# A convolution by pairs of images: the last pair computed with row products too, and work dealt out anew among VectorE, ScalarE and GpSimd

## The chip, the cores and the metric

One core of one Trainium2 chip. The metric is device time in microseconds of one execution of the whole kernel; lower is better.

## The reference

The input `x` has 32 images of 64 channels of 56 x 56 numbers, in float32. The weights `W` are 64 x 64 x 3 x 3, and only their signs are used.

```
bw  = sign(W)
g   = x.reshape(32, 32 groups, 2 channels, 56, 56)
xn  = (g - mean(g over channels, rows, columns)) / sqrt(var(g) + 1e-5)
out = x + conv2d(xn, bw, 3x3, stride 1, padding 1)
```

So each group of two neighbouring channels of an image is normalised by itself, convolved with weights of +1 and -1, and added to the input.

## The kernel before

**Pairs.** The 32 images are 16 pairs (`k` from 0 to 15, `LAST` is 15). A pair fills the 128 partitions, 64 channels of each image. It lies in one of `XRING` = 8 slots of `xbuf`, where the result is added in place and from where it is stored.

**Normalising.** For a pair, VectorE takes `bn_stats` of seven blocks (L500), combines them (`aggregate`, L502) and makes the factor and the offset (`scale`, L513), with a square root from ScalarE (`deviation`, L411) between. ScalarE then writes the scaled pair twice, as float16 (`hi`, L421, into `halves`) and as float32 (`normalise`, L415, into `xnorm`). GpSimd subtracts the one from the other (`lo`, L326), which gives a second float16 half, so that the convolution keeps its precision with float16 matmuls. This is done by chunks of rows (`chunks`, L132): two per pair, 29 and 27 rows in an ordinary pair. `halves` has three slots, `xnorm` two.

**Convolution.** TensorE runs 64x64 weight tiles, four at a time. A block of up to 9 rows takes 9 taps for the upper half and then 9 for the lower, added up in one PSUM bank. *Home* blocks write an image's result to its own partitions, *away* blocks to the other image's: rows are shared out between the two so that all four quarters of the array work. A block starts with the nine taps of the upper half, and waits for the lower one only then (`wait_lower`, L695). Home blocks use PSUM banks 0 to 3, away blocks 4 to 7, in units of two banks; a block of unit `u` waits in `wait_bank` (L669) until the unit `u - 2` on its side has been read out.

**Products.** In the pairs of `WINOGRAD` (L30: 3, 6, 9, 12, 14) the 18 rows 25 to 42 are computed as 9 couples of rows by four row products of three taps each, in place of 18 rows by nine taps. Their inputs are the lines STEP (even row minus odd), SUM (odd plus even) and DIFF (rows two apart), made by GpSimd from the raw input (`make_lines`, L347), scaled twice by ScalarE (`line_upper`, L440, into `line_halves` and `lines_norm`) and subtracted by GpSimd (`lo_lines`, L363). The other 13 home rows are ordinary blocks, 25 rows are away. Such a pair has chunks of 26 and 14 rows, since rows between are needed only as lines. In L78 the unit of the 13 rows comes first, then products 2 and 1, then 0 and 3.

**Taking the result out.** VectorE adds home blocks from PSUM to `xbuf` (`add_home` L546; `add_inner` L589 and `add_outer` L602 for the products). An away unit goes one of two ways (`by_scalar`, L115): VectorE adds it in two operations of 64 partitions (`add_away`, L559), or ScalarE moves it across partitions to `moved` (`move_away`, L427) and GpSimd adds it (`add_away`, L333). Before the change the second unit of an ordinary pair and the first of a product pair go by ScalarE and GpSimd, the rest by VectorE.

**Order.** Each engine's program is written out by hand, pair by pair, and runs in order; engines meet at counting semaphores. VectorE works on statistics two pairs ahead. SyncE issues all loads and stores, three in flight (`load`, `paced_store`), with those of the last pair after L308. TensorE deals a pair's home and away steps alternately by columns done (L746). In the last pair the blocks get narrower towards the end (L76, L83), so that little is left to add and store after the last matmul.

## Time and profile before

| | us |
|---|---|
| median of 3 runs | 201.85 (201.57 to 202.32) |
| span of the profiled execution | 200.7 |
| PE busy | 191.2 (95%) |
| DVE busy | 165.3 (82%) |
| ACT busy | 149.7 (75%) |
| POOL busy | 166.7 (83%) |
| granted TensorE clock | 1.00 of full speed |

The span runs from the first instruction to the last of one profiled execution, and is 1.15 us shorter than the median of the runs. PE is TensorE, DVE is VectorE, ACT is ScalarE and POOL is GpSimd. PEld is TensorE's loading of weights, which runs beside its matmuls. In rows of the trace, L followed by a number is a line of the kernel, `out<-in` names the tiles, and the bracket at the end says how long the engine had stood idle before and what ended that.

### The profile page before, as it was taken

Reading aid. Unit: us, or ns where it says so; the run is one execution under the profiler, and the core shown is the slowest. Engines: PE = TensorE matmul, PEld = TensorE weight load, DVE = VectorE, ACT = ScalarE, POOL = GpSimd, SP = SyncE. Lnnn points to the kernel's source line nnn. Section 1 sums busy time; section 2 is a strip of 40 time slices with the busy share of each in tenths; the row PEclk is TensorE's granted clock in tenths of the full one; section 3 lists DMA queues with packets and bytes.
Section 4 is the critical chain, followed back from the end, with each engine's and each line's share of the span. In section 5 each row is a group of like instructions: output and inputs, shape, how many; then the busy total and the mean of one; then the engine's idle time right before and its main releaser. Section 6 shows DMA issues by size and latency. Waiting matters only on the chain.

```text
span 200.7 us, 10042 instructions
## 1 busy us (share of the span) xinstructions
PE 191.2 (95%) x4482; PEld 168.4 (84%) x4482; DVE 165.3 (82%) x363; ACT 149.7 (75%) x142; POOL 166.7 (83%) x85
## 2 busy tenths in 40 slices
PE   1999999999999999999999999999999999999990
PEld 0478888879858988988999988899998999889990
DVE  2799999996999997799988779998779999627392
ACT  3185999799989289899909989972998999595000
POOL 1029786999999999999999997999999899999500
PEclk9999999999999999999999999999999999999999
DMA  6978977871787988868697887868887883906274
GB/s 216 362 217 292 331 246 252 289 209 44 306 243 291 297 316 282 282 248 278 242 301 296 275 327 276 325 228 321 326 241 296 266 319 152 381 13 238 116 283 175
DMA packets 18698, 52.17 MB, mean 260 GB/s; under 512 B 2080, under 2 KB 5024, under 8 KB 18656
## 3 DMA queue, kind: packets, MB, share of 16 engines
q1 hardware_dynamic: 18656, 51.54, 72.9%
q8 instruction: 35, 0.57, 1.1%
q14 instruction: 7, 0.06, 0.1%
HBM read 25.84 MB, written 25.69 MB: 257 GB/s over the span
## 4 chain that ended last, share of the span: by engine, by line
PE 65%; ACT 14%; DVE 13%; DMA 3%; issue 1%; SPq 0%; DVEq 0%; ACTq 0%
PE psum L738 65%; ACT halves L424 5%; DVE stats L500 5%; ACT xnorm L418 4%; DMA xbuf<-in_x_dram 3%; ACT moved L437 3%; DVE xbuf L570 2%; DVE xbuf L556 1%; DVE xbuf L580 1%; DVE own L508 1%; ACT line_halves L447 1%; ACT std L413 1%; DVE xbuf L544 1%; ACT lines_norm L451 1%; DVE halves L538 1%
## 5 line engine op out<-in xcount | busy, mean ns | idle before, releaser
L738 PE MATMUL psum<-halves,w_taps 64*64 64x385 f16 (+8 forms) x4140 | 183.4, 325 | 0.5 <-DVE halves L532 0.4
L738 PEld LDWEIGHTS psum<-halves,w_taps 64*64 64x64 f16 x4140 | 156.7, 107 | 19.3 <-ACT moved L437 0.9
L330 POOL TENSOR_TENSOR halves<-xnorm,halves 128x784 f16<-128x784 f32 (+5 forms) x35 | 91.6, 2637 | 20.0 <-ACT xnorm L418 19.7
L500 DVE BATCH_NORM_STATS2 stats<-xbuf 128x6 f32<-128x448 f32 x112 | 60.8, 613 | 4.3 <-DMA xbuf<-in_x_dram 4.1
L424 ACT ACTIVATE halves<-xbuf,coef 128x784 f16<-128x784 f32 (+5 forms) x35 | 50.7, 1449 | 3.0 <-DVE coef L525 2.8
L418 ACT ACTIVATE xnorm<-xbuf,coef 128x784 f32<-128x784 f32 (+5 forms) x35 | 50.5, 1443 | 0.0
L437 ACT ACTIVATE moved<-psum 64x784 f32<-64x784 f32 (+1 forms) x30 | 25.5, 850 | 7.9 <-PE psum L738 7.3
L345 POOL TENSOR_TENSOR xbuf<-xbuf,moved 128x784 f32<-128x784 f32 (+1 forms) x15 | 29.3, 1956 | 0.4 <-ACT moved L437 0.4
L570 DVE SCALAR_TENSOR_TENSOR xbuf<-psum,xbuf 64x784 f32<-64x784 f32 (+1 forms) x32 | 28.2, 881 | 1.0
L556 DVE SCALAR_TENSOR_TENSOR xbuf<-psum,xbuf 128x784 f32<-128x784 f32 x21 | 20.3, 967 | 7.6 <-PE psum L738 7.4
L371 POOL TENSOR_TENSOR line_halves<-lines_norm,line_halves 128x1512 f16<-128x1512 f32 (+1 forms) x10 | 20.9, 2120 | 0.5 <-ACT lines_norm L451 0.5
L738 PE MATMUL psum<-line_halves,w_products 64*64 64x504 f16 (+1 forms) x180 | 20.8, 373 | 0.0
L587 DVE SCALAR_TENSOR_TENSOR xbuf<-psum,xbuf 128x504 f32<-128x504 f32 x30 | 18.6, 673 | 1.5 <-PE psum L738 1.5
L413 ACT ACTIVATE std<-own,eps 128x1 f32<-128x1 f32 x16 | 4.6, 287 | 14.8 <-DVE own L508 14.8
L358 POOL TENSOR_TENSOR lines<-xbuf 128x1008 f32<-128x1008 f32 x5 | 11.7, 2337 | 0.0
L651 PE MATMUL psum<-filler 64*64 64x448 f16 x84 | 7.3, 508 | 4.2 <-DMA xbuf<-in_x_dram 4.2
L544 DVE SCALAR_TENSOR_TENSOR xbuf<-psum,xbuf 128x392 f32<-128x392 f32 (+3 forms) x13 | 6.2, 508 | 5.9 <-PE psum L738 5.8
L738 PEld LDWEIGHTS psum<-line_halves,w_products 64*64 64x64 f16 x180 | 10.0, 107 | 0.7
L651 PEld LDWEIGHTS psum<-filler 64*64 64x64 f16 x84 | 3.5, 154 | 7.1 <-DMA xbuf<-in_x_dram 4.2
L508 DVE BATCH_NORM_AGGREGATE own<-stats 128x2 f32<-128x84 f32 x16 | 8.5, 534 | 0.6
L517 DVE RECIPROCAL inv<-std 128x1 f32<-128x1 f32 x16 | 2.6, 161 | 7.1 <-ACT std L413 7.1
L451 ACT ACTIVATE lines_norm<-lines,coef 128x1512 f32<-128x1512 f32 x5 | 7.7, 1542 | 0.0
(36 smaller groups left out, 72.0 us busy)
## 6 DMA issues: line engine op xcount, KB each, us to landing
xbuf<-in_x_dram SPq DMA_DIRECT2D x48, 448.0 KB, 4.6
out_dram<-xbuf SPq DMA_DIRECT2D x43, 392.0 KB, 4.0
xbuf<-in_x_dram SPq DMA_DIRECT2D x16, 224.0 KB, 4.1
out_dram<-xbuf SPq DMA_DIRECT2D x5, 504.0 KB, 3.9
out_dram<-xbuf SPq DMA_DIRECT2D x5, 448.0 KB, 3.8
out_dram<-xbuf SPq DMA_DIRECT2D x5, 364.0 KB, 4.1
out_dram<-xbuf SPq DMA_DIRECT2D x5, 252.0 KB, 4.1
out_dram<-xbuf SPq DMA_DIRECT2D x1, 224.0 KB, 3.8
```

What stands on the lines that cost most here:

```text
L330: nc.gpsimd.tensor_tensor(at(halves[:, k % HRING, 1, :], a, b), at(xnorm[:, k % NRING, :], a, b), at(halves[:, k % HRING, 0, :], a, b), AL ...
L345: nc.gpsimd.tensor_tensor(away, away, part, ALU.add).then_inc(add_done, 1)
L358: nc.gpsimd.tensor_tensor(lines[:, DIFF], at(xbuf[:, s, :], WROW - 1, WROW + WROWS - 1), at(xbuf[:, s, :], WROW + 1, WROW + WROWS + 1), AL ...
L371: nc.gpsimd.tensor_tensor(line_halves[:, 1, some], lines_norm[:, some], line_halves[:, 0, some], ALU.subtract).then_inc(line_lo_ready, 1)
L418: nc.scalar.activation(at(xnorm[:, k % NRING, :], a, b), at(xbuf[:, s, :], a, b), ACT.Identity, bias=coef[:, s, 1:2], scale=coef[:, s, 0:1 ...
L424: nc.scalar.activation(at(halves[:, k % HRING, 0, :], a, b), at(xbuf[:, s, :], a, b), ACT.Identity, bias=coef[:, s, 1:2], scale=coef[:, s, ...
L437: nc.scalar.mul(moved[here, m % 2, 0:len(unit) * size].rearrange("p (n m) -> p n m", m=size), psum[there, bank:bank + len(unit), 0:size], ...
L500: nc.vector.bn_stats(stats[:, n, :], xbuf[:, s, n * STAT:(n + 1) * STAT]).then_inc(blocks_ready, 1)
L556: nc.vector.scalar_tensor_tensor(both_rows, psum[:, bank:bank + 2, 0:BN], 1.0 / SCALE, both_rows, ALU.mult, ALU.add).then_inc(home_done, 1)
L570: nc.vector.scalar_tensor_tensor(part[here], made[there], 1.0 / SCALE, part[here], ALU.mult, ALU.add).then_inc(away_done, 1)
L587: return nc.vector.scalar_tensor_tensor(part, made, factor / SCALE, part, ALU.mult, ALU.add)
L738: mm = pe.matmul(outs[:, :, left:right], weights, ins[:, :, left + dx:right + dx], start=first_step, stop=last_step)
```

## The change

It has four parts.

1. **The last pair is a product pair** (`WINOGRAD` gets 15). Its home units are 7 rows, products 2 and 1, products 0 and 3, then 3 and 3 rows; its away units 16, 6 and 3 rows. Its stores are cut to match, and its chunks are 26 and 14 rows.
2. **Lines.** SUM is made by VectorE (`sum_line`), with twice the mean taken off in the same operation, so that all four quarter lines are scaled in one operation of 2016 elements. They are scaled in place (no `lines_norm`), and `lines` and `line_halves` are double. In pairs 14 and 15 VectorE makes the lower half of the lines itself, in one operation that also scales (`lo_lines` of VectorE); in the others GpSimd does, in one operation of 2016 elements where there were two of 1512 and 504.
3. **Away units.** All go by ScalarE and GpSimd, except those in `BY_VECTOR` and the last pair's. On both engines the add or move of a pair's first unit stands between the two chunks of the next pair (after them, if that is a product pair).
4. **VectorE's order.** The seven blocks of statistics are spread around the additions (4 and 3, or 2, 2 and 3), and `aggregate` comes after `add_inner` in a product pair.

`SCALAR_BLOCKS` is empty, so `stats_by_scalar` issues nothing and all statistics stay with VectorE.

```diff
-WINOGRAD = (3, 6, 9, 12, 14)
+WINOGRAD = (3, 6, 9, 12, 14, 15)
+LINES_BY_VECTOR = (14, 15)
+BY_VECTOR = {(0, 0), (1, 0), (13, 1), (14, 0), (14, 1)}
+SCALAR_BLOCKS = {}
...
     def home_units(k):
         if k == LAST:
-            return [[(0, 7), (14, 7)], [(28, 7), (42, 4)], [(50, 3)]]
+            return [[(WROW + WROWS, 7)], [2, 1], [0, 3], [(WROW + WROWS + 7, 3)], [(WROW + WROWS + 10, 3)]]
...
     def away_units(k):
         if k == LAST:
-            return [[(7, 7), (21, 7)], [(35, 7), (46, 4)], [(53, 3)]]
+            return [[(0, 8), (8, 8)], [(16, 6)], [(22, 3)]]
...
     def by_scalar(k, i):
-        return k != LAST and i == (0 if k in WINOGRAD else 1)
+        return k != LAST and (k, i) not in BY_VECTOR
...
 (SyncE, store_unit)
+                if k == LAST:
+                    wait_away(k, 0)
+                    store(k, 0, 0, 16)
+                    sp.wait_ge(home_done, home_before(k) + 3)
+                    store(k, 1, WROW, WROW + WROWS + 7)
+                    sp.wait_ge(home_done, home_before(k) + 4)
+                    wait_away(k, 1)
+                    store(k, 2, 16, 22)
+                    store(k, 3, WROW + WROWS + 7, WROW + WROWS + 10)
+                    sp.wait_ge(home_done, home_before(k) + 5)
+                    store(k, 4, WROW + WROWS + 10, H)
+                    wait_away(k, 2)
+                    sp.dma_start(at(both(out, k), 22, WROW),
+                                 at(xbuf[:, k % XRING, :], 22, WROW)).then_inc(last_stored, 16)
+                    return
...
 (GpSimd, make_lines)
-                nc.gpsimd.tensor_tensor(lines[:, SUM].rearrange("p (r w) -> p r w", w=W), odd, even,
-                                        ALU.add).then_inc(lines_made, 1)
...
 (GpSimd, lo_lines)
-                for i, some in enumerate((slice(0, 3 * WN), SUM)):
-                    pool.wait_ge(line_hi_ready, 2 * n + i + 1)
-                    pool.wait_ge(line_norm_ready, 2 * n + i + 1)
-                    nc.gpsimd.tensor_tensor(line_halves[:, 1, some], lines_norm[:, some], line_halves[:, 0, some],
-                                            ALU.subtract).then_inc(line_lo_ready, 1)
+                pool.wait_ge(line_norm_ready, lines_before(k + 1, False))
+                nc.gpsimd.tensor_tensor(line_halves[:, n % 2, 1, :], lines[:, n % 2, :], line_halves[:, n % 2, 0, :],
+                                        ALU.subtract).then_inc(line_lo_pool, 1)
...
 (GpSimd, the loop over pairs)
             for k in range(NP):
-                if k >= 2 and k - 2 not in WINOGRAD and k != WINOGRAD[0]:
+                if k >= 2 and by_scalar(k - 2, 1):
                     add_away(k - 2, 1)
-                for c in range(len(chunks(k))):
+                last = len(chunks(k)) - 1
+                for c in range(last):
                     if (k, c) != (0, 0):
                         lo(k, c)
+                if k in WINOGRAD:
+                    lo(k, last)
+                if k >= 1 and by_scalar(k - 1, 0):
+                    add_away(k - 1, 0)
+                if k not in WINOGRAD:
+                    lo(k, last)
+                elif k not in LINES_BY_VECTOR:
+                    lo_lines(k)
...
 (ScalarE, line_upper)
+                nc.scalar.activation(line_halves[:, n % 2, 0, :], lines[:, n % 2, :], ACT.Identity,
+                                     scale=coef[:, k % XRING, 0:1]).then_inc(line_hi_ready, 1)
+                if k not in LINES_BY_VECTOR:
+                    act.wait_ge(line_hi_ready, n + 1)
+                    nc.scalar.activation(lines[:, n % 2, :], lines[:, n % 2, :], ACT.Identity,
+                                         scale=coef[:, k % XRING, 0:1]).then_inc(line_norm_ready, 1)
...
 (VectorE)
+            def sum_line(k):
...
+                nc.vector.scalar_tensor_tensor(lines[:, n % 2, SUM].rearrange("p (r w) -> p r w", w=W),
+                                               pairs_of_rows[:, :, 0:W], coef[:, s, 2:3], pairs_of_rows[:, :, W:],
+                                               ALU.add, ALU.add).then_inc(sum_made, 1)
+            def lo_lines(k):
...
+                nc.vector.scalar_tensor_tensor(line_halves[:, n % 2, 1, :], lines[:, n % 2, :], coef[:, k % XRING, 0:1],
+                                               line_halves[:, n % 2, 0, :], ALU.mult, ALU.subtract).then_inc(line_lo_ready, 1)
...
 (VectorE, the loop over pairs)
+                if k >= 1:
+                    if k - 1 in WINOGRAD:
+                        add_outer(k - 1)
+                    else:
+                        add_home(k - 1, 1)
+                    if not by_scalar(k - 1, 1):
+                        add_away(k - 1, 1)
+                if k in LINES_BY_VECTOR:
+                    lo_lines(k)
+                if k + 1 in WINOGRAD:
+                    sum_line(k + 1)
...
+            add_away(LAST, 0)
+            add_outer(LAST)
+            add_home(LAST, 3)
+            add_away(LAST, 1)
+            add_home(LAST, 4)
+            add_away(LAST, 2)
```

The lines in round brackets are not part of the diff and say where a piece stands.

Where the instructions of GpSimd stand, first from pair 5's lower halves to the lower half of pair 6's lines in the kernel before (`128x1624`, `128x1512` are the chunks of an ordinary pair, `128x1456`, `128x784` those of a product pair):

```order
L330 TENSOR_TENSOR halves<-xnorm,halves 128x1624
L330 TENSOR_TENSOR halves<-xnorm,halves 128x1512
L356 TENSOR_TENSOR lines<-xbuf 128x504
L358 TENSOR_TENSOR lines<-xbuf 128x1008
L360 TENSOR_TENSOR lines<-xbuf 128x504
L345 TENSOR_TENSOR xbuf<-xbuf,moved 128x2x392
L330 TENSOR_TENSOR halves<-xnorm,halves 128x1456
L330 TENSOR_TENSOR halves<-xnorm,halves 128x784
L371 TENSOR_TENSOR line_halves<-lines_norm,line_halves 128x1512
L371 TENSOR_TENSOR line_halves<-lines_norm,line_halves 128x504
```

The same stretch in the changed kernel:

```order
L397 TENSOR_TENSOR xbuf<-xbuf,moved 128x504
L382 TENSOR_TENSOR halves<-xnorm,halves 128x1624
L397 TENSOR_TENSOR xbuf<-xbuf,moved 128x2x392
L382 TENSOR_TENSOR halves<-xnorm,halves 128x1512
L409 TENSOR_TENSOR lines<-xbuf 128x504
L411 TENSOR_TENSOR lines<-xbuf 128x1008
L397 TENSOR_TENSOR xbuf<-xbuf,moved 128x2x392
L382 TENSOR_TENSOR halves<-xnorm,halves 128x1456
L382 TENSOR_TENSOR halves<-xnorm,halves 128x784
L397 TENSOR_TENSOR xbuf<-xbuf,moved 128x2x392
L418 TENSOR_TENSOR line_halves<-lines,line_halves 128x2016
```

Three additions of away rows have come in (pair 3's second unit, pair 4's first, pair 5's first), and the making of SUM has gone.

The second place is VectorE from the first additions of pair 14 into the last pair. Before (`128x9x56` is an addition of one product, `64x...` half of an away unit; six product additions in a row are four of `add_inner` and two of `add_outer`):

```order
L544 SCALAR_TENSOR_TENSOR xbuf<-psum,xbuf 128x392
L544 SCALAR_TENSOR_TENSOR xbuf<-psum,xbuf 128x336
L587 SCALAR_TENSOR_TENSOR xbuf<-psum,xbuf 128x9x56 x6
L570 SCALAR_TENSOR_TENSOR xbuf<-psum,xbuf 64x504 x2
L556 SCALAR_TENSOR_TENSOR xbuf<-psum,xbuf 128x2x392
```

And in the changed kernel:

```order
L712 SCALAR_TENSOR_TENSOR line_halves<-lines,coef,line_halves 128x2016
L702 SCALAR_TENSOR_TENSOR lines<-xbuf,coef 128x504
L631 SCALAR_TENSOR_TENSOR xbuf<-psum,xbuf 128x392
L631 SCALAR_TENSOR_TENSOR xbuf<-psum,xbuf 128x336
L660 SCALAR_TENSOR_TENSOR xbuf<-psum,xbuf 64x896 x2
L667 SCALAR_TENSOR_TENSOR xbuf<-psum,xbuf 128x9x56 x6
L660 SCALAR_TENSOR_TENSOR xbuf<-psum,xbuf 64x504 x2
L712 SCALAR_TENSOR_TENSOR line_halves<-lines,coef,line_halves 128x2016
L631 SCALAR_TENSOR_TENSOR xbuf<-psum,xbuf 128x392
L667 SCALAR_TENSOR_TENSOR xbuf<-psum,xbuf 128x9x56 x4
L660 SCALAR_TENSOR_TENSOR xbuf<-psum,xbuf 64x896 x2
L667 SCALAR_TENSOR_TENSOR xbuf<-psum,xbuf 128x9x56 x2
```

Pair 14's first away unit (`64x896`) now stands ahead of its products, and the lower half of the last pair's lines behind its last away unit.

## Rows read from the trace of the kernel before

**Rows 1.** The page: span; busy time, share, count by engine

```profile
span 200.7 us, 10042 instructions
...
PE 191.2 (95%) x4482; PEld 168.4 (84%) x4482; DVE 165.3 (82%) x363; ACT 149.7 (75%) x142; POOL 166.7 (83%) x85
```

**Rows 2.** Timeline of weight loads, pairs 3 to 4 (start, length, instruction)

```profile
58.59 0.11 PEld L738 LDWEIGHTS psum<-halves,w_taps 64*64 64x64 f16 x2 [0.54 <-DVE xbuf L587]
59.05 0.97 PEld L738 LDWEIGHTS psum<-halves,w_taps 64*64 64x64 f16 x28 [0.35 <-ACT moved L437]
```

**Rows 3.** Stretch, length; busy us of PE, PEld, DVE, ACT, POOL; clock; DMA

```profile
92.50:127.00 34.50, 34.50 (x818) 31.78 (x812) 30.27 (x69) 28.27 (x26) 32.21 (x15) 1.00 0.83 291
```

**Rows 4.** Timeline of ScalarE: moves that waited for a pair's last matmul

```profile
139.40 1.66 ACT L437 ACTIVATE moved<-psum 64x784 f32<-64x784 f32 x2 [1.35 <-PE psum L738]
...
151.22 1.66 ACT L437 ACTIVATE moved<-psum 64x784 f32<-64x784 f32 x2 [0.69 <-PE psum L738]
...
173.55 1.66 ACT L437 ACTIVATE moved<-psum 64x784 f32<-64x784 f32 x2 [1.35 <-PE psum L738]
```

**Rows 5.** Timeline of GpSimd

```profile
33.00 6.31 POOL L330 TENSOR_TENSOR halves<-xnorm,halves 128x1624 f16<-128x1624 f32 x2 [1.54 <-ACT xnorm L418]
...
54.50 1.88 POOL L345 TENSOR_TENSOR xbuf<-xbuf,moved 128x784 f32<-128x784 f32 x1
56.33 6.34 POOL L330 TENSOR_TENSOR halves<-xnorm,halves 128x1624 f16<-128x1624 f32 x2
62.61 2.11 POOL L345 TENSOR_TENSOR xbuf<-xbuf,moved 128x896 f32<-128x896 f32 x1
64.68 6.30 POOL L330 TENSOR_TENSOR halves<-xnorm,halves 128x1624 f16<-128x1624 f32 x2
70.94 1.27 POOL L356 TENSOR_TENSOR lines<-xbuf 128x504 f32<-128x504 f32 x1
...
74.46 1.25 POOL L360 TENSOR_TENSOR lines<-xbuf 128x504 f32<-128x504 f32 x1
75.68 1.86 POOL L345 TENSOR_TENSOR xbuf<-xbuf,moved 128x784 f32<-128x784 f32 x1
77.50 4.61 POOL L330 TENSOR_TENSOR halves<-xnorm,halves 128x1456 f16<-128x1456 f32 x2
82.04 4.19 POOL L371 TENSOR_TENSOR line_halves<-lines_norm,line_halves 128x1512 f16<-128x1512 f32 x2
86.16 1.89 POOL L345 TENSOR_TENSOR xbuf<-xbuf,moved 128x784 f32<-128x784 f32 x1
...
169.43 4.62 POOL L330 TENSOR_TENSOR halves<-xnorm,halves 128x1456 f16<-128x1456 f32 x2
```

**Rows 6.** Groups of GpSimd by shape: busy, mean ns, idle before

```profile
L371 POOL TENSOR_TENSOR line_halves<-lines_norm,line_halves 128x1512 f16<-128x1512 f32 x5 | 15.4, 3079 | 0.5 <-ACT lines_norm L451 0.5
...
L371 POOL TENSOR_TENSOR line_halves<-lines_norm,line_halves 128x504 f16<-128x504 f32 x5 | 5.8, 1161 | 0.0
```

**Rows 7.** Timeline of VectorE in the last two pairs

```profile
178.92 0.98 DVE L544 SCALAR_TENSOR_TENSOR xbuf<-psum,xbuf 128x392 f32<-128x392 f32 x2 [4.50 <-PE psum L738]
180.14 2.55 DVE L587 SCALAR_TENSOR_TENSOR xbuf<-psum,xbuf 128x504 f32<-128x504 f32 x4 [0.24 <-PE psum L738]
183.97 1.27 DVE L587 SCALAR_TENSOR_TENSOR xbuf<-psum,xbuf 128x504 f32<-128x504 f32 x2 [1.28 <-PE psum L738]
...
195.95 0.33 DVE L544 SCALAR_TENSOR_TENSOR xbuf<-psum,xbuf 128x168 f32<-128x168 f32 x1
```

**Rows 8.** Groups of VectorE by shape: additions of away rows

```profile
L570 DVE SCALAR_TENSOR_TENSOR xbuf<-psum,xbuf 64x784 f32<-64x784 f32 x22 | 21.4, 973 | 0.7
...
L570 DVE SCALAR_TENSOR_TENSOR xbuf<-psum,xbuf 64x504 f32<-64x504 f32 x10 | 6.8, 680 | 0.3
```

**Rows 9.** Timeline: VectorE's one long operation on two SBUF inputs, and GpSimd

```profile
13.04 1.03 DVE L538 TENSOR_TENSOR halves<-xnorm,halves 128x840 f16<-128x840 f32 x1
...
14.00 1.69 POOL L330 TENSOR_TENSOR halves<-xnorm,halves 128x784 f16<-128x784 f32 x1 [12.64 <-ACT xnorm L418]
```

More of the change, by code:

```diff
@@ L550, in add_home @@
                 if k in WINOGRAD:
-                    (first, rows), (second, fewer) = home_units(k)[i]
-                    add_rows(k, bank, first, rows)
-                    add_rows(k, bank + 1, second, fewer).then_inc(home_done, 1)
+                    *begun, (j, (first, rows)) = enumerate(home_units(k)[i])
+                    for before, (first_before, rows_before) in begun:
+                        add_rows(k, bank + before, first_before, rows_before)
+                    add_rows(k, bank + j, first, rows).then_inc(home_done, 1)
                     return
@@ L697, in wait_lower @@
                 if b.product is not None:
[L698 removed]
+                    wait_lines(pe, k)
                 elif (k, last_chunk(b)) == (0, 0):
```

216 lines of the change are left out of this document (130 added, 86 removed).

## The prediction, made before the change was run

> **What bounds the kernel now.** I read the page first. TensorE is busy 95% of the span [rows 1], and from its first convolution at 12 us to its last at 196 us the trace shows one real stop. It is at the seam of pairs 3 and 4 [rows 2]: 0.54 us until VectorE's product additions free a PSUM bank, then 0.35 us for a move by ScalarE, 0.9 us together. Everything else is matmul work. ScalarE's moves that waited for a pair's last matmul give its pace [rows 4]: an ordinary pair takes 151.22 - 139.40 = 11.82 us; pairs 12 and 13 take 22.33 us, so a product pair takes 10.51; a cycle of two ordinary pairs and one product pair takes 34.15.
>
> So the other engines cost nothing as long as they keep up, and the question to the trace is who is nearest to not doing so. In a stretch of 34.5 us GpSimd is busy 32.2, VectorE 30.3, ScalarE 28.3 [rows 3]. GpSimd's timeline says it sharper [rows 5]: from 54.50 to 86.16, pairs 4 to 6, it works without a gap, 31.66 us for a cycle in which TensorE needs 34.15. Its reserve is 2.5 us in each cycle, and it is spent in waiting for work. At the end the margin is visible: the second chunk's lower half of pair 14 is ready at 169.43 + 4.62 = 174.05 [rows 5]. Pair 13 ends for ScalarE at 173.55 [rows 4], pair 14's first matmul is some 0.3 us before that, and its nine upper taps of 392 columns take 1.5 us at 2.4 GHz, so TensorE asks for it at 174.7. It is 0.65 us early.
>
> **The last pair as a product pair** saves TensorE 11.82 - 10.51 = 1.3 us.
>
> **GpSimd.** From starts in its gapless stretch [rows 5]: the two lower halves of an ordinary pair take 6.28 us (56.33 to 62.61), those of a product pair 4.54 (77.50 to 82.04), adding 784 elements 1.82 (75.68 to 77.50), adding 896 2.07 (62.61 to 64.68), STEP and DIFF 3.52 (70.94 to 74.46), SUM 1.22, both lower halves of the lines 4.12. Two sizes are new. Adding 504: 0.25 us for 112 elements, so 1.2. One operation of 2016 elements: 1512 take 3.08 and 504 take 1.16 [rows 6], so 1.90 ns each and 4.04, less the 0.05 by which neighbours overlap: 3.99. The bounds are 3.8, the slope without a fixed part, and 4.24, both rows together.
>
> The Trainium skill (GPSIMD Engine Reference, Performance versus the Vector engine) gives 4497 ns for a float32 `tensor_tensor` of 2048 elements. By it an operation of 2016 would be about 4.4 us, an estimate, and the four of them would add 1.6 us; this trace's own rows are faster per element and decide.
>
> A cycle of the changed kernel, pairs 4 to 6:
>
> - pair 4: 1.82 + 6.28 + 2.07 = 10.17
> - pair 5: 1.22 + 6.28 + 1.82 + 3.52 = 12.84
> - pair 6: 1.82 + 4.54 + 1.82 + 3.99 = 12.17
>
> That is 35.18 us against TensorE's 34.15. **GpSimd becomes the bound**: what came in is two additions of 784 and one of 504 (4.86), what went is SUM and a fixed part (1.35).
>
> Followed from 33.00, where the lower halves of pair 2 start when ScalarE has delivered [rows 5], which nothing ahead of it changes: pair 2 with pair 3's STEP and DIFF 9.80, pair 3 12.17, three cycles 105.54, pair 13 1.82 + 6.28 + 2.07 + 3.52 = 13.69, pair 14 until its second chunk 1.22 + 4.54 = 5.76. Sum 146.96, so 179.96, where TensorE asked for it at 174.7. **TensorE is 5.3 us late** there. The stalls on the way (about 1.1 us in each of pairs 3, 6, 9 and 12, before the lower half of the product of STEP, and some 2 us in pair 14's first block) are this same lateness. The 0.9 us at pair 4 is swallowed by it too.
>
> **ScalarE** gets two moves of 1.66 us [rows 4] and a shorter one of about 1.2 per cycle, less 0.8 for merged lines: 28.3 + 3.7 = 32 of 34.15. It stays under, and GpSimd, being later, hides it. **VectorE** loses eight units of 2 us and four of 1.4 and gets pair 13's second (2.0) and pair 14's first (2.1); it is no bound until pair 14. **Statistics and SUM** cost nothing, since VectorE has this room.
>
> **The last two pairs, on VectorE.** Before, it adds pair 14's 13 home rows from 178.92, its products from 180.14, its outer products from 183.97 when the pair is done [rows 7]. All shift by 5.3. An away half of 784 takes 0.97, of 504 0.68 [rows 8], so one of 896 takes 1.09. The lower half of 2016 line elements is a new operation: with the slope of those two rows, 1.0 ns, it takes 2.2; the bounds are half of that and 3.3.
>
> - Home rows 184.2 to 185.1. The away unit of 16 rows, 64% of the pair, is ready at 185.5 and takes until 187.5. Only then come the four inner products, 2.4 us, to 189.9. The last pair's first block waits for their bank. Pair 14's last matmul is issued at 173.2 + 10.5 + 5.3 = 189.0: **stall 0.9**, and the last pair starts at 189.9.
> - Outer products 1.2, away unit 1.3, lower half of the lines 2.2: done at 194.6. After 7 rows (3.0 us) and three upper taps of 504 (0.65) TensorE wants it at 193.55: **stall 1.05**.
> - The last block, 3 rows, needs the bank of products 0 and 3. VectorE takes the inner products from 195.3 with a wait, to 197.9, the 16 away rows to 199.9, the outer products to 201.1. TensorE would come there at 189.9 + 10.6 + 1.05 - 1.3 = 200.25: **stall 0.85**. Its last 1.3 us with the end of the last matmul bring 202.65.
> - Then the tail. Before, VectorE's last home addition starts at 195.95 [rows 7] and the span ends at 200.7, 4.75 later. As many operations and a store of 3 rows follow here: 207.4.
>
> As differences: 5.3 + 0.9 + 1.05 + 0.85 - 1.3 = 6.8, rounded the same way. The profiled execution lies 1.15 us under the median, and that stays: 207.4 + 1.15 gives **208.5 us**, 3.3% slower.
>
> **Stores and loads.** The DMA share is 0.83 in the middle [rows 3], and away rows reach SyncE up to 5 us later. With loads three pairs ahead I cost that at nothing; without this cover a load would be late for the statistics, worth up to 2 us.
>
> **Rivals.**
>
> *Contention.* `sum_line` and the new `lo_lines` read two SBUF inputs on VectorE. The only long operation of that kind before ran at 13.04 to 14.07, while GpSimd stood idle until 14.00 [rows 9], so the trace is silent. If GpSimd stopped for as long, that is five times 0.68 [rows 8] before pair 14, 3.4 us: 211.9. The Trainium skill (GPSIMD Engine Reference, Specifications) says that GpSimd's SBUF interfaces are shared with VectorE, with contention when VectorE has two SBUF inputs or a 2-port mode. No row here shows it. Chance 0.10.
>
> *Stores late*, as above, up to 210.5: 0.07.
>
> *GpSimd keeps up.* If it is 3.6% faster than its rows (146.96 down to 141.7), its lateness vanishes. VectorE's three stalls (2.8) stay, the last pair gives 1.3 and the seam at pair 4 gives 0.9: 201.85 + 2.8 - 2.2 = 202.45, up to 203.5 where GpSimd is just at the edge. For it speaks that its spans are rough; against it, that I took starts, not spans. Chance 0.10.
>
> *Faster.* VectorE's additions slow GpSimd now, and it quickens once VectorE has lost them. The place is every cycle, the price the 5.3 us, and it decides the sign only if VectorE's chain also shortens, with the 2016 elements in 1.1 us and the away unit of pair 14 at the same quicker rate: then 201.85 - 1.3 - 0.9 = 199.7. Against it: GpSimd's addition of 784 takes 1.86 to 1.89 in all of [rows 5], whatever VectorE does beside it. Chance 0.05.
>
> **How the numbers follow.** The forecast has 0.68. Its unknown costs are 0.2 less or more for each of the four operations of 2016 on GpSimd, 1.1 for VectorE's, and 1% on GpSimd's 147 us (a pair of lower halves is 6.30 to 6.34 in [rows 5]), 1.5 us. Together that is 205.1 to 211.9 at the outside. The range of 205.5 to 211.5 holds nearly all of it and most of the first two rivals, and leaves out the last two and a full contention. A measurement can tell 0.5% (1 us) from no change: faster 0.05, same 0.04 (the lower half of the third rival), slower 0.91.
>
> **What would show it.** GpSimd should have no gap over 0.2 us from 33 us to about 190, its operation of 2016 should take 4.0 us, and the second chunk of pair 14 should be ready near 180. TensorE should stop about 1.1 us in each of pairs 6, 9 and 12 on GpSimd, some 2 us in pair 14, and about 1 us three times in the last pair on VectorE. Idle time on GpSimd in the middle, or operations clearly shorter than before, would prove the forecast wrong; operations longer only beside `sum_line` would be the contention.

## The result, and the profile after

| | before | after |
|---|---|---|
| median, us | 201.71 (201.52 to 202.32) | 228.69 (228.13 to 230.19) |
| ratio, with 95% interval | 1 | 1.132 (1.128 to 1.136) |
| profiled execution: span, us | 200.7 | 228.4 |
| mean granted TensorE clock | 1.00 | 0.97 |

The sign was forecast, the size was not: 20 us are missing. The page of the kernel after, busy time by engine and the granted clock in 40 slices (against [rows 1]):

```profile
span 228.4 us, 9931 instructions
...
PE 197.3 (86%) x4422; PEld 164.8 (72%) x4422; DVE 189.5 (83%) x344; ACT 161.6 (71%) x152; POOL 176.7 (77%) x86
...
PEclk9999999999999997699999999999958999999999
```

VectorE lost additions and yet is busy 24 us longer. GpSimd, forecast to be full from 33 to 190 us, is busy 77%. Twice the clock falls. The groups of instructions of the same page name the operation (busy, mean ns, idle before):

```profile
L702 DVE SCALAR_TENSOR_TENSOR lines<-xbuf,coef 128x504 f32<-128x504 f32 x6 | 35.3, 5891 | 0.0
...
L667 DVE SCALAR_TENSOR_TENSOR xbuf<-psum,xbuf 128x504 f32<-128x504 f32 x36 | 22.4, 674 | 1.4 <-PE psum L853 1.4
L418 POOL TENSOR_TENSOR line_halves<-lines,line_halves 128x2016 f16<-128x2016 f32 x4 | 16.1, 4024 | 9.4 <-ACT lines L500 9.4
```

SUM, 504 elements on VectorE, takes 5.9 us in the mean; an addition of the same 504 with one input in PSUM and one in SBUF keeps its 0.67. The mean hides two kinds of execution. VectorE's timeline (start, length, instruction) around pair 6, in pair 9, and in pair 12:

```profile
71.92 0.96 DVE L644 SCALAR_TENSOR_TENSOR xbuf<-psum,xbuf 128x784 f32<-128x784 f32 x1
72.80 13.96 DVE L702 SCALAR_TENSOR_TENSOR lines<-xbuf,coef 128x504 f32<-128x504 f32 x1
86.68 2.19 DVE L581 BATCH_NORM_STATS2 stats<-xbuf 128x6 f32<-128x448 f32 x4
88.80 0.95 DVE L644 SCALAR_TENSOR_TENSOR xbuf<-psum,xbuf 128x784 f32<-128x784 f32 x1
...
116.57 1.91 DVE L702 SCALAR_TENSOR_TENSOR lines<-xbuf,coef 128x504 f32<-128x504 f32 x1
...
151.73 13.95 DVE L702 SCALAR_TENSOR_TENSOR lines<-xbuf,coef 128x504 f32<-128x504 f32 x1
```

And GpSimd's timeline beside it:

```profile
71.48 3.10 POOL L382 TENSOR_TENSOR halves<-xnorm,halves 128x1512 f16<-128x1512 f32 x1
74.50 1.30 POOL L409 TENSOR_TENSOR lines<-xbuf 128x504 f32<-128x504 f32 x1
75.71 2.37 POOL L411 TENSOR_TENSOR lines<-xbuf 128x1008 f32<-128x1008 f32 x1
77.99 1.90 POOL L397 TENSOR_TENSOR xbuf<-xbuf,moved 128x784 f32<-128x784 f32 x1
79.80 4.63 POOL L382 TENSOR_TENSOR halves<-xnorm,halves 128x1456 f16<-128x1456 f32 x2
84.33 1.89 POOL L397 TENSOR_TENSOR xbuf<-xbuf,moved 128x784 f32<-128x784 f32 x1
90.92 4.02 POOL L418 TENSOR_TENSOR line_halves<-lines,line_halves 128x2016 f16<-128x2016 f32 x1 [4.70 <-ACT lines L500]
...
114.86 3.08 POOL L382 TENSOR_TENSOR halves<-xnorm,halves 128x1512 f16<-128x1512 f32 x1
117.88 1.72 POOL L409 TENSOR_TENSOR lines<-xbuf 128x504 f32<-128x504 f32 x1
```

SUM starts at 72.80 and ends at 86.76, 0.54 us after GpSimd's seven operations in a row ended at 86.22 and GpSimd had nothing more to do. In pair 9 it starts at 116.57, under GpSimd's lower half, ends at 118.48, 0.54 after that one's end (117.94), and GpSimd's next operation, STEP, takes 1.72 in place of 1.30. So one waits for the other, and in pairs 6 and 12 SUM was passed over until GpSimd's row of operations broke off. "Idle 0.0" stands before it: the profile counts such a wait as busy time of VectorE.

Who waits behind it is in the waits of the whole span (total, times, longest), and in the timeline of weight loads:

```profile
PEld psum L853 <- DVE xbuf L644: 13.4, 2, 6.7
PE psum L853 <- DVE xbuf L644: 12.6, 2, 6.3
POOL line_halves L418 <- ACT lines L500: 9.4, 2, 4.7
...
ACT line_halves L496 <- DVE lines L702: 6.8, 1, 6.8
```

```profile
89.80 6.24 PEld L853 LDWEIGHTS psum<-halves,w_taps 64*64 64x64 f16 x90 [6.71 <-DVE xbuf L644]
```

The statistics and the home addition of pair 5 stand behind SUM on VectorE, so TensorE gets no free PSUM bank from 83.1 to 89.8. GpSimd's lower half of the lines waits for ScalarE, which waits for SUM. Windows on both sides of the stop (stretch, length; busy us and count of PE, PEld, DVE, ACT, POOL; clock; DMA):

```profile
83.20:89.60 6.40, 0.28 (x8) 0.00 (x0) 6.40 (x6) 2.71 (x2) 3.02 (x2) 0.89 0.42 158
90.00:94.00 4.00, 4.00 (x50) 3.18 (x52) 3.61 (x12) 2.61 (x4) 3.08 (x1) 0.50 0.86 286
96.00:100.00 4.00, 4.00 (x98) 3.47 (x93) 2.00 (x5) 2.25 (x2) 3.11 (x2) 1.00 0.02 5
```

After 6.4 us without work TensorE runs at half clock, 1.2 GHz, 50 matmuls in 4 us where later there are 98. By the times of the matmuls, pair 5 takes 18.4 us for 11.8, pair 6 13.1 for 10.5, and pairs 11 and 12 the same: 18.0 us more in these four. Pair 14 takes 5.6 more, pairs 3 and 9 2.7, the last pair 1.4.

### The profile page after: what moved, and what is told of

Its sections match the earlier page's. It is cut to its first block, busy times and chain, and to the rows that moved or that the text cites. A ratio compares the mean times of both kernels' runs of the same rounds, so it can differ in the third digit from the quotient of the medians.

```text
span 228.4 us, 9931 instructions
## 1 busy us (share of the span) xinstructions
PE 197.3 (86%) x4422; PEld 164.8 (72%) x4422; DVE 189.5 (83%) x344; ACT 161.6 (71%) x152; POOL 176.7 (77%) x86
## 4 chain that ended last, share of the span: by engine, by line
DVE 33%; ACT 20%; PE 17%; POOL 16%; issue 8%; DMA 3%; SPq 0%; DVEq 0%; ACTq 0%; POOLq 0%
PE psum L853 17%; DVE lines L702 13%; POOL halves L382 9%; ACT halves L473 7%; ACT xnorm L467 7%; DVE stats L581 5%; ACT moved L486 5%; POOL line_halves L418 3%; DVE xbuf L660 3%; DMA xbuf<-in_x_dram 3%; DVE line_halves L712 2%; POOL xbuf L397 2%; DVE xbuf L667 2%; DVE xbuf L644 2%; DVE xbuf L631 1%
## 5 line engine op out<-in xcount | busy, mean ns | idle before, releaser
L853 PE MATMUL psum<-halves,w_taps 64*64 64x385 f16 (+6 forms) x4032 | 189.3, 331 | 17.0 <-DVE xbuf L644 12.6
L853 PEld LDWEIGHTS psum<-halves,w_taps 64*64 64x64 f16 x4032 | 155.0, 109 | 40.8 <-DVE xbuf L644 13.4
L486 ACT ACTIVATE moved<-psum 64x784 f32<-64x784 f32 (+2 forms) x50 | 39.8, 797 | 9.6 <-PE psum L853 8.4
L397 POOL TENSOR_TENSOR xbuf<-xbuf,moved 128x784 f32<-128x784 f32 (+2 forms) x25 | 45.3, 1813 | 0.8 <-ACT moved L486 0.7
L702 DVE SCALAR_TENSOR_TENSOR lines<-xbuf,coef 128x504 f32<-128x504 f32 x6 | 35.3, 5891 | 0.0
L853 PE MATMUL psum<-line_halves,w_products 64*64 64x495 f16 (+1 forms) x216 | 25.7, 374 | 3.2 <-POOL line_halves L418 1.9
L496 ACT ACTIVATE line_halves<-lines,coef 128x2016 f16<-128x2016 f32 x6 | 11.9, 1976 | 17.7 <-DVE lines L702 6.8
L418 POOL TENSOR_TENSOR line_halves<-lines,line_halves 128x2016 f16<-128x2016 f32 x4 | 16.1, 4024 | 9.4 <-ACT lines L500 9.4
L606 DVE RECIPROCAL inv<-std 128x1 f32<-128x1 f32 x16 | 2.6, 164 | 15.3 <-ACT std L462 15.0
L660 DVE SCALAR_TENSOR_TENSOR xbuf<-psum,xbuf 64x784 f32<-64x784 f32 (+4 forms) x16 | 13.2, 826 | 0.5
L631 DVE SCALAR_TENSOR_TENSOR xbuf<-psum,xbuf 128x392 f32<-128x392 f32 (+2 forms) x13 | 6.1, 501 | 8.4 <-PE psum L853 8.4
L853 PE MATMUL psum<-line_halves,w_taps 64*64 64x495 f16 (+1 forms) x72 | 8.7, 373 | 1.5 <-DVE xbuf L631 1.5
```

The costliest lines, as they stand in the source:

```text
L397: nc.gpsimd.tensor_tensor(away, away, part, ALU.add).then_inc(add_done, 1)
L418: nc.gpsimd.tensor_tensor(line_halves[:, n % 2, 1, :], lines[:, n % 2, :], line_halves[:, n % 2, 0, :], ALU.subtract).then_inc(line_lo_poo ...
L486: nc.scalar.mul(moved[here, m % 2, 0:len(unit) * size].rearrange("p (n m) -> p n m", m=size), psum[there, bank:bank + len(unit), 0:size], ...
L660: nc.vector.scalar_tensor_tensor(part[here], made[there], 1.0 / SCALE, part[here], ALU.mult, ALU.add).then_inc(away_done, 1)
L702: nc.vector.scalar_tensor_tensor(lines[:, n % 2, SUM].rearrange("p (r w) -> p r w", w=W), pairs_of_rows[:, :, 0:W], coef[:, s, 2:3], pairs ...
L853: mm = pe.matmul(outs[:, :, left:right], weights, ins[:, :, left + dx:right + dx], start=first_step, stop=last_step)
```

## The experiments

"Of the change" below means an edit of the kernel after, "of before" one of the kernel before. Ratios are to the kernel before, measured beside each. A time without an interval is that of one execution, or the middle of four that lie too far apart, which are then given.

**Theory A**: a VectorE operation with two SBUF inputs and a GpSimd operation exclude each other. Its rivals stand in the expectations.

**yield_for_sum**, of the change: GpSimd waits for SUM.

```diff
 (GpSimd, make_lines, ahead of STEP)
+                pool.wait_ge(sum_made, n + 1)
```

> The changed kernel, with one wait added: GpSimd starts STEP only when VectorE's SUM is made. In the changed kernel VectorE's SUM operation of 504 elements took 13.96 us in pairs 6 and 12 and 0.91 to 2.80 in the others, and TensorE stood 6.65 us each time behind it and then ran at half clock. Theory A (exclusion): VectorE's operation with two SBUF inputs cannot run beside a GpSimd operation and may be passed over as long as GpSimd's operations follow each other without a gap. Then the wait gives it a gap: all six SUM operations take under 4 us, the two stops of 6.65 us go with their half-clock stretches (some 18 us together), and the time is about 211 us. Theory B (the operation is slow by itself, by its access pattern or its place in SBUF): two operations of 14 us stay and the time stays at 228 or more. Theory C (DMA traffic holds it): as B.

213.43 us, 1.060 (1.053 to 1.067). The group of SUM:

```profile
L703 DVE SCALAR_TENSOR_TENSOR lines<-xbuf,coef 128x504 f32<-128x504 f32 x6 | 10.8, 1800 | 0.0
```

None is held past one GpSimd operation, the stops of 6.7 us and the half clock after them are gone: 15.3 us from one added line.

**before_two_inputs** and **before_one_input**, of before: five unused operations on VectorE where the change makes SUM. They differ in the number of SBUF inputs, and with it in the instruction.

```diff
 (VectorE, the loop over pairs, ahead of the statistics)
+                if k + 1 in WINOGRAD:
...
+                    nc.vector.scalar_tensor_tensor(extra[:, n, :].rearrange("p (r w) -> p r w", w=W), pairs_of_rows[:, :, 0:W],
+                                                       eps[:], pairs_of_rows[:, :, W:], ALU.add, ALU.add)
```

In the second, `tensor_scalar(extra..., pairs_of_rows[:, :, 0:W], -1.0, 0.0, ALU.mult, ALU.add)` stands there.

> The kernel before, with five operations more on VectorE, at the places where the changed kernel makes SUM: 504 elements, two SBUF inputs, result not used. Theory A: each lasts until GpSimd's running operation ends (1 to 4 us), and one or more may be passed over for a whole row of GpSimd operations, over 6 us; GpSimd's operation beside each is longer by about 0.45 us; the time rises above 203 us. Theory B: all take the same time, whether GpSimd is busy or not. If the operation costs only its own 0.67 us, the time stays at 201.7.

> The kernel before, with five operations more on VectorE at the same places: 504 elements, one SBUF input (float32, times -1), result not used. Theory A, if a second SBUF input is what matters: all take 0.4 to 0.7 us and the time stays within 0.5% of 201.7. If an operation with one float32 SBUF input that runs at two elements per cycle needs the same interface, as the Trainium skill says (GPSIMD Engine Reference, Specifications), they are as long as those with two inputs.

With two inputs 215.63 us, 1.068 (1.064 to 1.073); with one 201.87, 1.000 (0.998 to 1.003). The groups of the added operations, of the one and of the other:

```profile
L633 DVE SCALAR_TENSOR_TENSOR extra<-xbuf,eps 128x504 f32<-128x504 f32 x5 | 21.7, 4341 | 0.0
```

```profile
L633 DVE TENSOR_SCALAR extra<-xbuf 128x504 f32<-128x504 f32 x5 | 3.4, 671 | 0.0
```

VectorE's timeline with two inputs, TensorE's weight loads behind it, and GpSimd's last operations before its pause:

```profile
71.31 15.22 DVE L633 SCALAR_TENSOR_TENSOR extra<-xbuf,eps 128x504 f32<-128x504 f32 x1
```

```profile
91.15 0.13 PEld L746 LDWEIGHTS psum<-halves,w_taps 64*64 64x64 f16 x2 [9.23 <-DVE xbuf L557]
```

```profile
77.30 4.59 POOL L331 TENSOR_TENSOR halves<-xnorm,halves 128x1456 f16<-128x1456 f32 x2
81.86 4.13 POOL L372 TENSOR_TENSOR line_halves<-lines_norm,line_halves 128x1512 f16<-128x1512 f32 x2
```

Nearly all of the 14 us is one operation that nobody reads: held for 15.22, again until 0.54 after GpSimd's end (85.99), with a stop of 9.2 us on TensorE. By the matmuls, pairs 5 and 6 take 14.0 us more. The other four took 1.3 to 2.4. The same place with one input costs nothing, and the instruction is not the reason, since the additions are `scalar_tensor_tensor` too and keep their 0.67 with one input in PSUM. So the inputs are the cause, and nothing else of the change is needed for it.

**away_as_before**, of the change: away units dealt as before. **relieved**: that and (13, 1) by VectorE, the lines of pair 14 by GpSimd.

```diff
-BY_VECTOR = {(0, 0), (1, 0), (13, 1), (14, 0), (14, 1)}
+BY_VECTOR = {(k, 1 if k in WINOGRAD else 0) for k in range(15)}
```

```diff
-LINES_BY_VECTOR = (14, 15)
+LINES_BY_VECTOR = (15,)
-BY_VECTOR = {(0, 0), (1, 0), (13, 1), (14, 0), (14, 1)}
+BY_VECTOR = {(k, 1 if k in WINOGRAD else 0) for k in range(15)} | {(13, 1)}
```

> The changed kernel with its away units dealt as before the change (the first of an ordinary and the second of a product pair by VectorE, all pairs but the last). GpSimd has some 5 us less per cycle and VectorE has them more. Theory A: GpSimd has gaps again, from which SUM profits only if one comes in time, so that no SUM lasts over 7 us; time 203 to 215 us. Theory D (the time is lost because GpSimd has too much to do, as in the forecast, and SUM's length is only a symptom): time about 203 us.

> The changed kernel with its away units dealt as before the change but pair 13's second by VectorE, and the lower half of pair 14's lines by GpSimd, so that VectorE has only one long two-input operation left (pair 15's) beside the six of SUM. If no SUM is passed over, what stays against the kernel before is a wait of some 2 us at the start of the last pair and 1 us at its end, less 1.3 us of matmuls and the 0.9 us at pair 4: 201.5 to 204 us. If one is passed over, 208 us or more.

212.97 us, 1.052 (1.047 to 1.058), and 205.92, 1.021 (1.018 to 1.024), which is over the 201.5 to 204 expected. With GpSimd's reserve back, TensorE has no stop over 0.5 us from 15 to 172 us in either. What is left of the loss is in the last two pairs: by the matmuls 8.6 and 1.8 us in away_as_before, with five stops of 1.3 to 2.7 us and a half-clock stretch, and VectorE's operation of 2016 elements at 3.99 us beside GpSimd (2.32 alone). In relieved it is 2.3 and 1.8 us, and the largest stops are 1.90, 1.92 and 1.26:

```profile
PEld psum L853 <- DVE xbuf L660: 2.1, 2, 1.9
...
PEld psum L853 <- DVE line_halves L712: 1.9, 1, 1.9
```

That is the best version with products in the last pair, and it is still behind the kernel before. Its stalls there (between 5 and 6 us) are more than the 1.3 us that the products save.

**away_dealt_anew**, of before: only the new dealing and the new order, no operation with two SBUF inputs added; GpSimd still makes SUM. It leaves out adding rows 8 to 15 of pair 14's first away unit.

```diff
 (by_scalar; the orders of GpSimd, ScalarE and VectorE's statistics as in the change)
-        return k != LAST and i == (0 if k in WINOGRAD else 1)
+        return k != LAST and (k, i) not in {(0, 0), (1, 0), (13, 1), (14, 0), (14, 1)}
```

> The kernel before with the away units dealt as in the change, and VectorE's statistics and the orders of ScalarE and GpSimd as in the change, but with its own lines, all by GpSimd, its own last pair and no operation with two SBUF inputs on VectorE. The forecast's mechanism alone: GpSimd's cycle is 31.66 + 4.86 = 36.5 us against TensorE's 34.15, so TensorE loses about 2.4 us a cycle and some 12 us in all: 212 to 215 us, with GpSimd without gaps. If GpSimd's load is not what the forecast took it for, the time stays near 202.

215.88 us, 1.069 (1.066 to 1.073). The wait that TensorE got, and two of its stops:

```profile
PEld psum L746 <- POOL halves L330: 12.9, 9, 3.9
```

```profile
86.44 3.86 PEld L746 LDWEIGHTS psum<-halves,w_taps 64*64 64x64 f16 x98 [1.93 <-POOL halves L330]
122.91 3.86 PEld L746 LDWEIGHTS psum<-halves,w_taps 64*64 64x64 f16 x98 [1.93 <-POOL halves L330]
```

The stops come 36.5 us apart, as expected for GpSimd's cycle here (1.22 and a fixed part more than in the change's), so TensorE loses 2.3 us in each, expected 2.4. The sums over GpSimd's rows hold. Why the time lies 0.9 us over the expected 212 to 215 is open; the largest stop, 3.86 us, is in pair 14.

**one_input_lines**, of the change: its two kinds of operation on VectorE with one SBUF input. It leaves out the even rows of SUM, and the subtraction in the lines of pairs 14 and 15.

```diff
 (sum_line; lo_lines likewise, over 2016 elements)
-                nc.vector.scalar_tensor_tensor(lines[:, n % 2, SUM].rearrange("p (r w) -> p r w", w=W),
-                                               pairs_of_rows[:, :, 0:W], coef[:, s, 2:3], pairs_of_rows[:, :, W:],
-                                               ALU.add, ALU.add).then_inc(sum_made, 1)
+                nc.vector.tensor_scalar(lines[:, n % 2, SUM].rearrange("p (r w) -> p r w", w=W),
+                                        pairs_of_rows[:, :, 0:W], coef[:, s, 2:3], 0.0,
+                                        ALU.add, ALU.add).then_inc(sum_made, 1)
```

> The changed kernel with VectorE's SUM and lower half of the lines each made by an operation with one SBUF input (it leaves the even rows out of SUM and the subtraction out of the lower half in pairs 14 and 15), same tiles and counts otherwise. Theory A (exclusion of two-input operations): SUM takes 0.7 us in all six pairs, no stop of 6.6 us, and what is left is the forecast's sum less some 0.9 us for the quicker lower half: about 207.5 us. Theory B or C (the place of the tile, the strided access, DMA traffic): SUM stays at up to 14 us and the time near 228.

216.58 us, 1.073 (1.069 to 1.077). Expected were 207.5. Up to 180 us it is the forecast: SUM takes 0.73, and TensorE stops about 1.2 us in pairs 3, 6, 9 and 12 and 1.8 in pair 14. Then a surprise on VectorE:

```profile
180.00 10.15 DVE L712 TENSOR_SCALAR line_halves<-lines,coef 128x2016 f16<-128x2016 f32 x1
190.07 0.72 DVE L702 TENSOR_SCALAR lines<-xbuf,coef 128x504 f32<-128x504 f32 x1
```

One SBUF input, and held past five operations of GpSimd. The same instruction takes 1.27 us in the last pair, 0.63 ns an element, where SUM's form over strided rows needs 1.45: a form at nearly double rate is excluded too. **one_input_single_rate** cut it into four of 9 x 56, meant to be slow ones:

```diff
+                for q in range(4):
...
+                    step = nc.vector.tensor_scalar(lower, made, coef[:, k % XRING, 0:1], 0.0, ALU.mult, ALU.add)
+                step.then_inc(line_lo_ready, 1)
```

> As the run with one SBUF input, but the lower half of the lines in pairs 14 and 15 is written by four operations of 9 rows of 56 elements each (SUM's own shape, which took 0.73 us beside a busy GpSimd), in place of one of 2016 neighbouring elements, which was held for 10.15 us in pair 14 and took 1.27 us in pair 15 with GpSimd idle. It leaves out of SUM the even rows and out of the lower half the subtraction. If only two inputs or an operation at double rate are held, nothing is held here, the four take 2.6 us together, and the time is that of the forecast, 208.5 us (207.5 to 210). If any long VectorE operation can be held beside GpSimd, one of the four is, and the time is 212 or more.

217.49 us, 1.077 (1.073 to 1.081): the first was held 9.36, the free ones took 0.49 each, so they were no slow ones. The test missed its aim. **one_input_one_wait** is one_input_lines, with the same parts left out, and one wait, so that GpSimd yields to that operation too:

```diff
 (GpSimd, make_lines, ahead of STEP)
+                if k == LAST:
+                    pool.wait_ge(line_lo_ready, 1)
```

> As the run with one SBUF input (it leaves the even rows out of SUM and the subtraction out of the lower half of the lines in pairs 14 and 15), with one wait more: GpSimd makes the last pair's STEP only when VectorE has written pair 14's lower half. That takes away the one operation that was held there, for 10.15 us. What is left is the forecast's own sum: GpSimd's load, VectorE's late work in the last two pairs: 207 to 210 us. If the forecast's sum was wrong in itself, the time is outside this.

**208.44 us**, 1.031 (1.026 to 1.036). TensorE's stops on GpSimd by its weight loads:

```profile
54.60 0.11 PEld L855 LDWEIGHTS psum<-line_halves,w_products 64*64 64x64 f16 x2 [1.24 <-POOL line_halves L420]
89.70 0.11 PEld L855 LDWEIGHTS psum<-line_halves,w_products 64*64 64x64 f16 x2 [1.19 <-POOL line_halves L420]
...
179.36 3.86 PEld L855 LDWEIGHTS psum<-halves,w_taps 64*64 64x64 f16 x98 [1.83 <-POOL halves L382]
```

This is the changed kernel nearly without the exclusion: only pair 14's operation still waited for one of GpSimd's (2.14 us for 1.27). It lands near the forecast's sum, 208.5.

**two_inputs_every_pair** and **double_rate_every_pair**, of before: 13 unused operations, in pairs 2 to 14, of two inputs, or of one at double rate. Against before_two_inputs:

```diff
-                if k + 1 in WINOGRAD:
+                if k >= 2 and k + 1 < NP:
```

> The kernel before with the unused operation of 504 elements and two SBUF inputs on VectorE in each of pairs 2 to 14, thirteen in all, so as to see how often one is passed over. Theory A: each waits at least for the end of GpSimd's running operation; of twelve such operations seen so far with GpSimd busy three were passed over, so 1 to 5 of the thirteen last over 6 us, and each of those costs TensorE 6 us or more. If being passed over hangs on the operations that stand around it, as STEP and DIFF, only those ahead of a product pair are.

> The kernel before with an unused VectorE operation on one SBUF input of 504 neighbouring float32 elements in each of pairs 2 to 14. By the slope between 2016 elements in 1.27 us and 840 in 0.72 us it runs near two elements per cycle, 0.55 us when free. If the double rate is what takes GpSimd's interface, most of the thirteen last until the end of GpSimd's running operation, 0.6 to 3.7 us, and one or more may be passed over. If the 10.15 us had another cause, all thirteen take the same 0.5 to 0.6 us.

204.61 and 206.61 us, one execution each. Theory A alone would let such operations wait for one of GpSimd's, and here that is so: 0.7 to 2.7 us with two inputs, 0.42 free and up to 3.25 at double rate. None was held over 6 us, where one to five were expected, and thirteen of them cost less than five did.

So what decides whether one is held? **sum_one_later** and **sum_two_later**, of the change, put one or two blocks of statistics ahead of SUM, to move the moment at which it comes up:

```diff
+                if 1 <= k < NP - 2:
+                    pair_stats(k + 2, range(1))
                 if k + 1 in WINOGRAD:
                     sum_line(k + 1)
```

> The changed kernel with SUM one block of statistics (0.55 us) later on VectorE, nothing else moved. If being passed over is a matter of when the operation comes up against GpSimd's, the two pairs that were passed over (6 and 12) change: with none passed over, SUM takes 0.6 to 3.7 us everywhere and the time is 211 to 215; with one, about 220. If it belongs to these pairs (their slots of xbuf or of the lines), SUM takes 14 us in pairs 6 and 12 again and the time stays near 228.

> As the last, with SUM two blocks (1.1 us) later. The same two theories; by the first the pairs that are passed over are others or none, by the second 6 and 12.

228.55 us (221.07, 227.84, 229.26 and 229.46), and 228.27 in one execution. In the traces SUM is held in pairs 6 and 12 again, 13.4 and 12.9 us, until the same point of GpSimd's row: a shift of 0.6 or 1.1 us does not free it. But the 221.07 lies 7.5 us under the middle, and by an estimate one hold costs as much (15.1 us for the change's two, as worked out below). So one kernel may be held in one execution and not in another, and each trace here is of one execution; there is none of the short one. **line_slots_swapped** gives the pairs the other slot of `lines` (the line below, and likewise wherever a slot is chosen), **yield_in_two_pairs** lets GpSimd wait in pairs 6 and 12 alone, **small_gpsimd_op** puts a small memset ahead of STEP there:

```diff
-                made = lines[:, n % 2, :]
+                made = lines[:, 1 - n % 2, :]
```

```diff
+                if k in (6, 12):
+                    pool.wait_ge(sum_made, n + 1)
```

```diff
+                if k + 1 in (6, 12):
+                    nc.gpsimd.memset(unused[:, k:k + 1], 0.0)
```

> The changed kernel with the two slots of the lines swapped, so that pairs 3, 9 and 14 use the second and 6, 12 and 15 the first. SUM was passed over in pairs 6 and 12, both with the second slot, whenever it was issued. If the slot decides, it is passed over in 3, 9 or 14 and not in 6 and 12. If something else of these pairs decides, 6 and 12 stay as they are and the time is near 228.

> The changed kernel with GpSimd waiting for SUM in pairs 6 and 12 alone. Being passed over there costs the two stops of 6.65 us and the half-clock stretches behind them, 18 us by the two traces. If it happens in these pairs only, the time is 210 to 213 us and the rest of the trace is that of the changed kernel; if it comes up in another pair instead, 219 or more.

> The changed kernel with a tiny operation on GpSimd (a memset of one element per partition into an unused tile) between the last lower half of pairs 5 and 11 and the STEP of pairs 6 and 12. If VectorE's operation can come in wherever GpSimd's row is broken by something short or with other operands, SUM there takes 2 to 3 us and the time is about 211; if only a real pause lets it in, SUM stays at 13 to 14 us and the time near 228.

Swapped slots: 229.18 in one execution, pairs 6 and 12 still. Yield in two pairs: 236.76 us (221.45, 236.72, 236.81 and 237.54), where 210 to 213 was expected. In the trace, pairs 6 and 12 are free, but now SUM is held in pairs 9 and 14:

```profile
109.00 13.96 DVE L704 SCALAR_TENSOR_TENSOR lines<-xbuf,coef 128x504 f32<-128x504 f32 x1
...
179.04 16.93 DVE L704 SCALAR_TENSOR_TENSOR lines<-xbuf,coef 128x504 f32<-128x504 f32 x1
```

So it hangs on the pair no more than on the slot: giving way once moves it to later pairs. The memset, 219.71 in one execution: held in pair 6 (14.01), let in in pair 12 (2.31), right behind the memset.

A pattern runs through all traces so far. Each of the fourteen held operations came when GpSimd had worked 24 us or more without a pause and without having let one in. Of 69 that came within 12 us none was held, and none came between. Eight came at some 24 us or more and were let in: six where GpSimd was made to wait for VectorE's operation, and two with the memset (pairs 12 and 14). That suggested a pause of GpSimd, however short. **pause_at_step** and **pause_before**, of the change, let GpSimd wait for the end of its own operation before, at STEP, or some 6 us ahead of the moment when SUM comes up:

```diff
 (pause_at_step, GpSimd, ahead of make_lines; pair 15 on add_done)
+                        pool.wait_ge(lo_ready, chunks_by(k, last))
```

```diff
 (pause_before, GpSimd, after add_away(k - 2, 1))
+                    if k + 1 in WINOGRAD:
+                        pool.wait_ge(add_done, moves_before(away_before(k - 2) + 2))
```

> The changed kernel; GpSimd waits for the end of its own operation before each STEP, which parts the two by some 0.1 us, and for nothing else. Over all runs so far, VectorE's held operations came up when GpSimd had run for 24 us or more without a pause and without a VectorE operation let in between (nine times of ten), and never in the some forty that came up within 21 us. If any pause in GpSimd's row lets VectorE in, every SUM is let in at STEP at the latest and takes 0.7 to 3 us, and the time is 209 to 214 us. If the wait must be for VectorE's operation itself (as in yield_for_sum), SUM stays at 14 us in pairs 6 and 12 and the time near 228.

> The same short pause, but before the first lower half of the pair ahead of each product pair, 5 to 9 us before STEP; none at STEP. If the length of GpSimd's unbroken run decides, this breaks it well before SUM comes up, and SUM is let in at its first boundary as in pairs 3 and 9 of the changed kernel: 209 to 214 us. If a pause helps only while VectorE's operation is already waiting, SUM is passed over in pairs 6 and 12 and the time is near 228.

213.66 us, 1.056 (1.053 to 1.059), and 214.58, 1.062 (1.058 to 1.065); none held in either. In pause_before SUM comes up in pair 6 at 72.19, and GpSimd's timeline shows all of the pause, 64.62 + 1.27 = 65.89 to 65.97:

```profile
64.62 1.27 POOL L397 TENSOR_TENSOR xbuf<-xbuf,moved 128x504 f32<-128x504 f32 x1
65.97 3.29 POOL L382 TENSOR_TENSOR halves<-xnorm,halves 128x1624 f16<-128x1624 f32 x1
```

```profile
72.19 2.44 DVE L704 SCALAR_TENSOR_TENSOR lines<-xbuf,coef 128x504 f32<-128x504 f32 x1
```

0.08 us of GpSimd, 6 us ahead, and SUM waits 1.8 in place of 13.

## Why the prediction was wrong

**Right: GpSimd becomes the bound.** Its new operation took 4.02 us (forecast 4.04), TensorE's stops in pairs 3 and 9 of the change, 1.4 and 1.4 by the weight loads, and those of one_input_one_wait (1.17 to 1.24, and 1.83 in pair 14) are the forecast's 1.1 and some 2. There GpSimd's cycle is 35.1 us by the stops (54.60 to 89.70), forecast 35.18. The estimate of 4.4 us from the Trainium skill (GPSIMD Engine Reference, Performance versus the Vector engine) was too high, as the rows said. The page's figure is for float32, and the new operation has one float16 input; GpSimd's float32 additions (504 in 1.27, 896 in 2.11 us, [rows 5]) run at 2.1 ns an element, near the 2.2 that its figure gives (an estimate).

**Right in sum: the last two pairs.** In one_input_one_wait three stalls of 1.44, 0.39 and 1.26 us stood for the forecast ones (0.9, 1.05, 0.85), 3.1 for 2.8. The second is short because the lower half takes 1.27 us there. With two inputs and no GpSimd beside it that operation took 2.32 in away_as_before, forecast 2.2.

**The own part of the change** is about 208.44 less the 202.1 of the kernel before beside it, 6.3 us (1.031), forecast 6.65. That it is this close is in part luck: one_input_one_wait also has the quicker lower half, for which the expectation of one_input_lines took 0.9 us off, and it still has one wait on GpSimd in pair 14.

**The step that failed** is "*Statistics and SUM* cost nothing, since VectorE has this room", and the rival that should have carried it, *contention*. I priced that rival at "if GpSimd stopped for as long, that is five times 0.68": the wrong engine waiting, for the wrong length, at a chance of 0.10. It is VectorE that waits, for the whole of GpSimd's operation that runs (up to 3.3 us), GpSimd's next then waits its turn, and now and then VectorE waits for a whole row of operations. And VectorE was not free to wait: home additions stand behind SUM, and TensorE waits for the banks that they empty.

In sizes, from the medians (the kernel before took 201.7 to 202.3 beside them):

| | us | over the one above |
|---|---|---|
| before | 201.7 | |
| exclusion nearly taken out (one_input_one_wait) | 208.4 | 6.7 |
| exclusion, nothing held (yield_for_sum, pause_at_step) | 213.4, 213.7 | 5.1 |
| the change | 228.7 | 15.1 |

The 15 us are the two holds, with half clock behind each (14.5 us in pairs 5, 6, 11 and 12 by the matmuls of the two traces). The 5 us come from GpSimd, the bound, which has to wait for VectorE's turn in each cycle: in yield_for_sum TensorE waits 0.7 to 0.9 us for its lower halves ahead of the 1.36 of each product pair. A part of the 5 is the quicker lower half of one_input_one_wait: TensorE's stop for it in the last pair is 1.36 us in yield_for_sum and 0.39 there.

**The rule was there to be had.** [Rows 9] are silent on it, and I said so, then took the cheap price. The Trainium skill (SBUF — State Buffer, Summary: rules for kernel authors) says more than the sentence that I had weighed: where a VectorE instruction has two SBUF inputs and a GpSimd one reads SBUF, the second to issue blocks fully until the first is finished. The traces agree in pair 9 (1.91 us, up to GpSimd's end and 0.54 more). The rule accounts for the 213.5 and not for the 228.7: it has the second wait for one instruction, where pairs 6 and 12 show it waiting for seven.

**Left open:** by what rule VectorE is passed over. That a pause of 0.08 us prevents it is shown in two kernels, in all pairs of their traces, and none of their eight executions took over 215.0 us. That the length of GpSimd's unbroken work decides is a pattern with two exceptions, and the short executions of sum_one_later and yield_in_two_pairs speak for a part of chance. What a kernel with GpSimd's waits and the dealing of relieved would give was not tried.

## What to carry to other kernels

Before an operation is moved to VectorE, look at its inputs: two in SBUF, or one at double rate, meant waiting for whatever GpSimd ran, in every trace here. Every hold came while GpSimd worked without a pause, and a full GpSimd is the usual reason for moving an operation. Then either keep one input in PSUM, or give GpSimd a wait (on that operation, or on its own last one), and see what stands behind the operation on VectorE. And compare cycles before dealing work out: an engine with 2.5 us of reserve in 34 can't take 4.9 us and give 1.35.

## What the hardware showed unexpectedly

- VectorE's 504 elements with two SBUF inputs were held 13.96 and 13.95 us past seven GpSimd operations in the changed kernel, 15.22 as a single addition to the kernel before, 16.93 at the longest. They ended each time 0.54 us after GpSimd's last.
- The same happened to an operation with one SBUF input at 0.63 ns an element (10.15 us), and never to one at 1.45 (0.73 in all pairs). Additions with one input in PSUM kept their 0.67.
- A wait of GpSimd for its own operation before, 0.08 us ahead of each product pair, took 15 us off the kernel.
- Five unused operations slowed a kernel by 14 us. One of them was held, and TensorE's stop of 9.2 us was followed by 8 us at 1.2 GHz in place of 2.4.
